# Another order of slots within a step of a two-layer transformer kernel

## The chip, the cores and the metric

The kernel runs on one core of one Trainium2 chip. The metric is device time in microseconds (us), the median of the runs. Engines are called as in the profile: PE is TensorE (PEld its weight loads), DVE is VectorE, ACT is ScalarE, POOL is GpSimd, SP is SyncE, whose queue issues nearly all DMAs.

## The reference

Two transformer blocks with adaptive layer norm run one after the other on x of 16 batches x 256 rows x 256 features, 16 heads of 16 features. Layer 0 is causal and gated by a condition, layer 1 has a key mask. Cut to what matters:

```python
# layer 0
xm = layernorm(x) * g * (1 + sc_a) + (be * (1 + sc_a) + sh_a)      # modulated
q, k, v = split(xm @ Wqkv)                                          # 16 heads of 16
attn = softmax(where(causal, q @ k.T * 16**-0.5, -inf))
x = x + gt_a * (merge(attn @ v) @ Wproj + bproj)
xm = modulate(layernorm(x)); x = x + gt_m * (gelu(xm @ W1 + b1) @ W2 + b2)
# layer 1: the same without causal mask and gates, with biases on q, k, v and a key padding mask
```

## The kernel before, in words

Everything stays on the chip. Each layer has an attention part, a software pipeline over the 16 batches, and an MLP part, a pipeline over 8 chunks of two batches. The attention part is a loop over steps t. In step t five batches are at work, each at another stage: n = t is normalised and transposed, a = t-1 gets its q, k and v, b = t-2 its scores (for the row maxima), c = t-3 its transposed scores, exponentials and half of its product with v, d = t-4 the rest of that product, the division by the row sums, the output projection and the residual. A full step thus does one batch's worth of each stage.

A step is 16 slots, one for each head. In every slot PE issues the scores of one head of b (lines 591 and 592, in layer 1 line 595) and the transposed scores of one head (lines 608 to 610, in layer 1 line 614). What else comes in a slot is set by the table SLOT and by PV_SLOT (the products with v, in slots 1, 5, 9, 13). Each engine's program is a fixed list in slot order; engines wait for each other by semaphores alone. An engine whose next instruction waits does nothing behind it.

The pieces that SLOT places, each of them on PE and then on the engines that read its bank:

- xT: four transposes of xn (line 648) into g_bank1. ACT applies scale and shift to half f=0 in the same slot and to half f=1 in the next slot (line 872, two instructions each, a full copy and a rounded one), and POOL then subtracts the rounded copy from the full one (line 1276, the low part of the operand). Both parts make xmT, which q, k and v of the next step read.
- q and k, two halves of six matmuls each (line 542), into g_bank1 and g_bank0; after the second half ACT rounds (line 819 or 823), DVE takes the low part (line 1054 or 1058), and SP copies both into q_stack or k_stack by six DMAs (line 407). The first matmul of q waits for xmT (semaphore xmT_ready).
- v, two halves of six, into g_bank1, copied by ACT (line 857).
- negmaxT: two transposes of the negated row maxima, copied by ACT (line 838), written into q_stack by SP.
- oT: two sets of four transposes (line 686) of the attention output, into g_bank0 and g_bank1; for each DVE takes the reciprocal of the sums and multiplies (lines 1126 and 1128).
- attnT: four transposes of the result (line 694), split by ACT (line 863) and DVE (line 1133).
- proj: two halves of six matmuls (line 542) with the output weights; DVE adds the bias (line 1138), POOL applies the gate and adds to x (lines 1257 and 1260).

The two g banks are handed from piece to piece; `take` waits until the piece that had the bank before has been read. The scores have three banks and the transposed scores two, so PE may run ahead of DVE and ACT by so much.

Of the kernel before, what the change touches and what calls it, by code (L numbers as in the profile page):

```python
# [27 lines left out]
LAYERS, B, T, D = 2, 16, 256, 256  # L28
H, HD = 16, 16
F = 4 * D  # L30
P = 128
NF, NM, NT = D // P, F // P, T // P
# [5 lines left out]
NG = H // GROUP  # L38
# [5 lines left out]
S_BANK = [h % 3 for h in range(H - 1)] + [1]  # L44
S_AGO = [next(k for k in range(1, H) if S_BANK[h - k] == S_BANK[h]) for h in range(H)]

SLOT = {"q": (0, 1), "negmaxT": 1, "k": (3, 5), "v": (6, 7), "oT": (8, 9), "attnT": 11, "xT": 12, "proj": (14, 15)}
PV_SLOT = [(LAG + 5 + GROUP * i) % H for i in range(NG)]

HALF = 3 * HD  # L50
# [40 lines left out]
def wait(eng, sem, value):  # L91
    if value is not None:
        eng.wait_ge(sem, value)
# [22 lines left out]
def build(nc, x_in, cond_in, mask_in, wa_in, w1_in, w2_in, ada0_in, ada1_in, cols_in, rows_in, ident_in,  # L116
          tri_in, out):
    fp32, f32r, bf16 = mybir.dt.float32, mybir.dt.float32r, mybir.dt.bfloat16
    ALU, ACT, AX = mybir.AluOpType, mybir.ActivationFunctionType, mybir.AxisListType

    with ExitStack() as ctx:
# [15 lines left out]
        ident = sb("ident", [P, P])  # L137
# [11 lines left out]
        xn = sb("xn", [P, 2, NT, D])  # L149
# [5 lines left out]
        negmax = sb("negmax", [P, 2, NT, 2, H], f32r)  # L155
        negmaxT = sb("negmaxT", [32, T], f32r)
        o_sb = sb("o_sb", [P, 2, NG, T])
# [340 lines left out]
        def _(pe):  # L498
# [40 lines left out]
            def product(dst, weights, rows, f, tiles):  # L539

                for n, (i, j) in enumerate(TERMS):
# [4 lines left out]

            USES = [("q", 1, 1, q_lo, 1), ("negmaxT", 0, 3, negmaxT_copied, 1), ("k", 0, 1, k_lo, 1),
                    ("v", 1, 1, v_copied, 1), ("oT0", 0, 4, attn_ready, 2), ("oT1", 1, 4, attn_ready, 2),
                    ("attnT", 0, 4, attnT_lo, 1), ("xT", 1, 0, xm_high, 1), ("proj", 0, 4, y_copied, 1)]

            BANK_OF = {u[0]: u[1] for u in USES}

# [80 lines left out]
            def step(layer, t):  # L633
                n, a, b, c, d = (t - k for k in range(5))
                gn, ga, gb, gc, gd = (in_layer(layer, s) for s in (n, a, b, c, d))
                for s in range(H):
                    if b.within(B):
                        scores(layer, gb, s)
                    if s < LAG and d.within(B):
                        scoresT(layer, gd, s + H - LAG)  # L640
                    if s >= LAG and c.within(B):
                        scoresT(layer, gc, s - LAG)
                    if s == SLOT["xT"] and n.within(B):
                        pe.wait_ge(xn_ready, gn.count(1, 1))
                        bank = take(layer, t, "xT")
                        for f in range(NF):
                            for i in range(NT):
                                last = transpose(bank[:, f * T + i * P:f * T + (i + 1) * P],
                                                 xn[:, gn.mod(2), i, f * P:(f + 1) * P], ident[:])
                        last.then_inc(xT_ready, 1)  # L650
                    if s == SLOT["negmaxT"] and c.within(B):
                        pe.wait_ge(negmax_ready, gc.count(1, 1))
                        bank = take(layer, t, "negmaxT")
                        for i in range(NT):
                            src = negmax[:, gc.mod(2), i].bitcast(fp32).rearrange("p e s -> p (e s)")
                            last = transpose(bank[0:32, i * P:(i + 1) * P], src, ident[:])
                        last.then_inc(negmaxT_ready, 1)
                    for name, first, ready in (("q", 0, q_ready), ("k", D, k_ready)):
                        if s in SLOT[name] and a.within(B):
                            m = SLOT[name].index(s)  # L660
                            if m == 0:
                                bank = take(layer, t, name)
                                if name == "q":
                                    pe.wait_ge(xmT_ready, ga.count(1, 1))
                                    pe.wait_ge(wa_split, 2 * layer + 1)
                            last = project(g_bank[BANK_OF[name]], ga, first, m)
                            if m == NF - 1:
                                last.then_inc(ready, 1)
                    if s in SLOT["v"] and a.within(B):
                        i = SLOT["v"].index(s)  # L670
                        if i == 0:
                            take(layer, t, "v")
                        bank = g_bank[BANK_OF["v"]]
                        for f in range(NF):
                            last = product(bank[:, i * D:(i + 1) * D],
                                           [xmT[:, ga.mod(2), e, f, i * P:(i + 1) * P] for e in range(2)],
                                           [wa[:, e, f, 2 * D:3 * D] for e in range(2)], f, NF)
                        if i == NT - 1:
                            last.then_inc(v_ready, 1)
                    if s in SLOT["oT"] and d.within(B):  # L680
                        i = SLOT["oT"].index(s)
                        if i == 0:
                            pe.wait_ge(o_copied, gd.count(NG, NG))
                        bank = take(layer, t, f"oT{i}")
                        for r in range(NG):
                            last = transpose(bank[:, r * P:(r + 1) * P], o_sb[:, gd.mod(2), r, i * P:(i + 1) * P],  # L686
                                             ident[:])
                        last.then_inc(oT_ready, 1)
                    if s == SLOT["attnT"] and d.within(B):
                        pe.wait_ge(attn_ready, gd.count(2, 2))  # L690
                        bank = take(layer, t, "attnT")
                        for f in range(NF):
                            for i in range(NT):
                                last = transpose(bank[:, f * T + i * P:f * T + (i + 1) * P],  # L694
                                                 attn[:, i, f * P:(f + 1) * P], ident[:])
                        last.then_inc(attnT_ready, 1)
                    if s in SLOT["proj"] and d.within(B):
                        i = SLOT["proj"].index(s)
                        if i == 0:
                            pe.wait_ge(attnT_lo, gd.count(1, 1))  # L700
                            take(layer, t, "proj")
                        bank = g_bank[BANK_OF["proj"]]
                        for f in range(NF):
                            last = product(bank[:, i * D:(i + 1) * D],
                                           [attnT[:, e, f, i * P:(i + 1) * P] for e in range(2)],
                                           [wa[:, e, f, 3 * D:4 * D] for e in range(2)], f, NF)
                        if i == NT - 1:
                            last.then_inc(proj_ready, 1)
                    if s in PV_SLOT:
                        r = PV_SLOT.index(s)  # L710
                        g, on = (gc, c) if LAG + 5 + GROUP * r < H else (gd, d)
                        if on.within(B):
                            attend(layer, g, r)
                    if s == SLOT["xT"] and t.const == ATTN_END:
                        chunk_transposes(layer, Step(0))
# [226 lines left out]
        def _(dve):  # L942
# [138 lines left out]
            def step(layer, t):  # L1081
# [3 lines left out]
                for s in range(H):  # L1085
# [26 lines left out]
                        row_statistics(layer, n)  # L1112
                    if s == SLOT["k"][1] and a.within(B):
                        low(layer, ga, k_hi, k_lo, g_bank[0], k_split, NF)
                    if s == 7 and n.within(B):
                        row_normalise(layer, n)
                    if s in SLOT["oT"] and d.within(B):
                        i = SLOT["oT"].index(s)
                        dve.wait_ge(oT_ready, gd.count(2, i + 1))
                        if i == 0:  # L1120
                            wait(dve, attnT_ready, gd.count(1))
                            if layer == 0 and d.const == 0:
                                dve.wait_ge(gates_stored, 16)
                        o = g_bank[i][:].rearrange("p (h n) -> p h n", n=32)
                        wait(dve, attn_ready, gd.count(2, i))
                        v.reciprocal(rsum[:, i], o[:, :, HD]).then_inc(rsum_ready, 1)
                        dve.wait_ge(rsum_ready, gd.count(2, i + 1))
                        v.tensor_tensor(attn[:, i].rearrange("p (h n) -> p h n", n=HD), o[:, :, 0:HD],
                                        rsum[:, i].unsqueeze(2).to_broadcast((P, H, HD)), ALU.mult)\
                            .then_inc(attn_ready, 1)  # L1130
                    if s == SLOT["attnT"] and d.within(B):
                        dve.wait_ge(attnT_hi, gd.count(1, 1))
                        v.tensor_tensor(attnT[:, 1], g_bank[0][:].rearrange("p (f n) -> p f n", f=NF), attnT[:, 0],
# [253 lines left out]
```

## Time and profile before

| | |
|---|---|
| median of 3 runs | 1167.23 us (1160.99 to 1169.55) |
| the profiled execution | 1161.7 us, span 1159.9 us |
| mean granted PE clock | 0.967 |
| PE busy | 1074.2 us (93%) |
| DVE, ACT, POOL busy | 787.0, 619.9, 252.6 us |

The span has four parts: attention of layer 0 to about 395 us, its MLP to about 606 us, attention of layer 1 to about 960 us, its MLP to the end. PE is busy almost throughout; a line of a timeline gives the start, the time taken, the engine, the line of the kernel, the operation, and in brackets the idle time ahead of it with what ended it. Starts of PE instructions that follow each other tell what each costs; their ends overlap the next ones.

### The profile page before, as it was taken

Reading aid. Unit: us, or ns where it says so; the run is one execution under the profiler, and the core shown is the slowest. Engines: PE = TensorE matmul, PEld = TensorE weight load, DVE = VectorE, ACT = ScalarE, POOL = GpSimd, SP = SyncE. Lnnn points to the kernel's source line nnn. Section 1 sums busy time; section 2 is a strip of 40 time slices with the busy share of each in tenths; the row PEclk is TensorE's granted clock in tenths of the full one; section 3 lists DMA queues with packets and bytes.
Section 4 is the critical chain, followed back from the end, with each engine's and each line's share of the span. In section 5 each row is a group of like instructions: output and inputs, shape, how many; then the busy total and the mean of one; then the engine's idle time right before and its main releaser. Section 6 shows DMA issues by size and latency. Waiting matters only on the chain.

```text
span 1159.9 us, 24601 instructions
## 1 busy us (share of the span) xinstructions
PE 1074.2 (93%) x8972; PEld 941.0 (81%) x8972; DVE 787.0 (68%) x2379; ACT 619.9 (53%) x1255; POOL 252.6 (22%) x253
## 2 busy tenths in 40 slices
PE   3879999999998789999975899999999987999998
PEld 3768888998886578998874788888888756988997
DVE  5568888888874577656635778878787746566553
ACT  1146667666664644433322677777777666334431
POOL 5111221312111342233321111121212013121111
PEclk9789999999998899999987899999999999999999
DMA  7657767575850100000056664736466400010001
GB/s 216 107 76 120 135 124 132 94 122 103 177 78 12 46 15 10 10 10 15 15 85 160 86 83 76 94 64 98 66 93 77 59 2 1 19 37 19 19 19 37
DMA packets 50832, 81.52 MB, mean 70 GB/s; under 512 B 8916, under 2 KB 23476, under 8 KB 49620
## 3 DMA queue, kind: packets, MB, share of 16 engines
q1 hardware_dynamic: 49752, 78.37, 38.2%
q10 hardware_dynamic: 960, 1.57, 1.2%
q8 instruction: 72, 1.18, 0.5%
q14 instruction: 48, 0.39, 0.2%
HBM read 22.64 MB, written 8.44 MB: 27 GB/s over the span
## 4 chain that ended last, share of the span: by engine, by line
PE 83%; DVE 4%; DMA 4%; SPq 2%; ACT 2%; issue 2%; POOL 2%; ACTq 1%; POOLq 0%; DVEq 0%
PE g_bank L542 14%; PE st_bank L542 13%; PE o_bank L628 9%; PE o_bank L542 8%; PE s_bank L542 7%; PE s_bank L595 6%; PE st_bank L614 5%; PE st_bank L608 4%; PE s_bank L591 3%; PE st_bank L610 3%; PE g_bank L686 2%; DMA k_stack<-qk_split 2%; SPq L407 2%; PE g_bank L694 1%; PE st_bank L609 1%
## 5 line engine op out<-in xcount | busy, mean ns | idle before, releaser
L806 ACT ACTIVATE probs<-st_bank 128x384 f32<-128x384 f32 (+1 forms) x512 | 273.4, 548 | 142.4 <-PE st_bank L610 81.7
L909 ACT ACTIVATE probs<-st_bank,cols 128x512 f32<-128x512 f32 x128 | 87.9, 689 | 217.8 <-PE st_bank L542 191.4
L542 PE MATMUL st_bank<-qk_split,q_stack 128*128 128x512 f32 x768 | 187.2, 402 | 14.5 <-ACT probs L909 10.9
L1099 DVE CUSTOM_DVE_ANT_0 s_bank<-s_bank,tri_wide 128x128 f32<-128x128 f32 (+1 forms) x512 | 170.3, 387 | 37.0 <-PE s_bank L592 35.8
L1105 DVE TENSOR_REDUCE maxima<-s_bank 128x2 f32<-128x512 f32 x256 | 168.7, 685 | 39.4 <-PE s_bank L595 38.6
L542 PEld LDWEIGHTS st_bank<-qk_split,q_stack 128*128 128x128 f32 x768 | 144.8, 191 | 51.9 <-ACT probs L909 14.0
L595 PE MATMUL s_bank<-k_stack,q_stack 97*128 97x256 f32 x512 | 115.2, 308 | 16.5 <-DMA k_stack<-mask_dram 9.4
L542 PE MATMUL g_bank<-xmT,wa 128*128 128x256 f32 x768 | 123.8, 301 | 4.8 <-POOL xmT L1276 4.8
L628 PE MATMUL o_bank<-probs,v_sb 128*32 128x256 f32 (+1 forms) x2048 | 124.5, 361 | 1.6 <-ACT probs L806 1.6
L595 PEld LDWEIGHTS s_bank<-k_stack,q_stack 97*128 97x128 f32 x512 | 79.8, 194 | 42.8 <-issue 25.9
L1276 POOL TENSOR_TENSOR xmT<-xm_full,xmT 128x512 fp32r<-128x512 f32 x32 | 42.3, 1322 | 320.3 <-ACT xmT L872 320.3
L542 PEld LDWEIGHTS g_bank<-xmT,wa 128*128 128x128 f32 x768 | 106.4, 202 | 5.7 <-issue 5.2
L614 PE MATMUL st_bank<-q_stack,k_stack 99*128 99x256 f32 x512 | 103.6, 286 | 3.1 <-DMA q_stack<-negmaxT 2.6
L591 PE MATMUL s_bank<-k_stack,q_stack 97*128 97x256 f32 x256 | 89.3, 350 | 9.8 <-DMA k_stack<-qk_split 6.4
L1202 DVE TENSOR_TENSOR wm_f32r<-probs,k_stack 128x512 fp32r<-128x512 f32 x128 | 92.7, 724 | 4.4
L542 PE MATMUL s_bank<-q_stack,k_stack 128*128 128x256 f32 x512 | 95.1, 284 | 0.0
L542 PE MATMUL o_bank<-q_stack,k_stack 128*128 128x256 f32 x512 | 94.8, 283 | 0.0
L608 PE MATMUL st_bank<-q_stack,k_stack 99*128 99x256 f32 x256 | 86.7, 340 | 4.6 <-DMA q_stack<-negmaxT 4.3
L628 PEld LDWEIGHTS o_bank<-probs,v_sb 128*32 128x32 f32 x2048 | 53.7, 110 | 43.0 <-issue 6.8
L614 PEld LDWEIGHTS st_bank<-q_stack,k_stack 99*128 99x128 f32 x512 | 79.2, 191 | 6.7 <-DMA q_stack<-negmaxT 3.2
L542 PEld LDWEIGHTS s_bank<-q_stack,k_stack 128*128 128x128 f32 x512 | 81.5, 192 | 0.0
L542 PEld LDWEIGHTS o_bank<-q_stack,k_stack 128*128 128x128 f32 x512 | 80.0, 189 | 0.0
(113 smaller groups left out, 2076.7 us busy)
## 6 DMA issues: line engine op xcount, KB each, us to landing
q_stack<-qk_split SPq DMA_DIRECT2D x192, 128.0 KB, 4.6
k_stack<-qk_split SPq DMA_DIRECT2D x180, 128.0 KB, 6.2
gate_rows<-gate_dram SPq DMA_DIRECT2D x32, 128.0 KB, 3.5
w_dram<-w_in SPq DMA_DIRECT2D x8, 512.0 KB, 7.0
wm_f32r<-w_dram SPq DMA_DIRECT2D x4, 1024.0 KB, 9.1
out<-x_sb SPq DMA_DIRECT2D x8, 512.0 KB, 2.9
x_sb<-x_in SPq DMA_DIRECT2D x4, 512.0 KB, 7.2
k_stack<-qk_split ACTq DMA_DIRECT2D x12, 128.0 KB, 8.4
```

Source lines behind the costliest of these rows:

```text
L542: last = mm(dst, weights[i], rows[j], start=(f == 0 and n == 0), stop=(f == tiles - 1 and n == len(TERMS) - 1))
L591: mm(bank[:, P:3 * P], q[:, P:T], k, start=True, stop=False)
L595: last = mm(bank[:, i * T:(i + 1) * T], q[:, i * P:(i + 1) * P], k, start=True, stop=True)
L608: mm(bank[:, 0:T], k[:, 0:P], q, start=True, stop=False)
L614: last = mm(bank[:, i * T:(i + 1) * T], k[:, i * P:(i + 1) * P], q, start=True, stop=True)
L628: last = mm(o_bank[32 * j:32 * j + 32, lo:T], v_sb[:, g.mod(VBUFS), kt, h, :], probs[:, h % 8, kt * T:kt * T + T - lo], start=(kt == 0), s ...
L806: activation(probs[:, h % 8, 0:n], st_bank[h % 2][:, 0:n], ACT.Exp, scale=SCALE)\
L909: activation(h_full[:, m % 2], st_bank[m % 2][:, :], ACT.Gelu, bias=cols[:, cb + m:cb + m + 1])\
L1099: last = v.tensor_tensor_reduce(out=bank[:, keys], in0=bank[:, keys], in1=tri_wide[:, T - (i + 1) * P:T], scale=1.0, scalar=LOWEST, op0=AL ...
L1105: v.reduce_max(maxima[:, gb.mod(2), :, slot], bank[:].rearrange("p (i n) -> p i n", n=T), AX.X).then_inc(max_done, 1)
L1202: v.tensor_tensor(hT[1][:, :, m], h, hT[0][:, :, m], ALU.subtract).then_inc(m_hT, 1)
L1276: g_.tensor_tensor(xmT[:, gn.mod(2), 1], xm_full[:], xmT[:, gn.mod(2), 0], ALU.subtract)\
```

## The change

The table SLOT is another one:

- q goes from slots 0 and 1 to 0 and 2, v from 6 and 7 to 4 and 6; k stays in 3 and 5, negmaxT in 1.
- oT goes from slots 8 and 9 to slot 7, both sets in a row; on DVE both divisions follow each other there, and row_normalise goes from slot 7 to slot 8.
- attnT goes from 11 to 9, proj from 14 and 15 to 11 and 12, xT from 12 to 13 (on ACT from 12 and 13 to 13 and 14).
- Where a slot has both, PE issues projections ahead of transposes.

No instruction is added or taken away, and SP's list of DMAs is the same.

```diff
-SLOT = {"q": (0, 1), "negmaxT": 1, "k": (3, 5), "v": (6, 7), "oT": (8, 9), "attnT": 11, "xT": 12, "proj": (14, 15)}
+SLOT = {"q": (0, 2), "negmaxT": 1, "k": (3, 5), "v": (4, 6), "oT": 7, "attnT": 9, "proj": (11, 12), "xT": 13}
...
-                    ("attnT", 0, 4, attnT_lo, 1), ("xT", 1, 0, xm_high, 1), ("proj", 0, 4, y_copied, 1)]
+                    ("attnT", 0, 4, attnT_lo, 1), ("proj", 0, 4, y_copied, 1), ("xT", 1, 0, xm_high, 1)]
...
+                    if s == SLOT["oT"] and d.within(B):
+                        pe.wait_ge(o_copied, gd.count(NG, NG))
+                        for i in range(NT):
+                            bank = take(layer, t, f"oT{i}")
+                            for r in range(NG):
+                                last = transpose(bank[:, r * P:(r + 1) * P],
+                                                 o_sb[:, gd.mod(2), r, i * P:(i + 1) * P], ident[:])
+                            last.then_inc(oT_ready, 1)
...
-                    if s == 7 and n.within(B):
+                    if s == SLOT["oT"] and d.within(B):
+                        for i in range(NT):
+                            dve.wait_ge(oT_ready, gd.count(2, i + 1))
...
+                    if s == 8 and n.within(B):
                         row_normalise(layer, n)
```

The first place is PE's list at the turn from one step to the next, in layer 0. These are the last instructions ahead of the first matmul of q (g_bank<-xmT,wa, which waits for xmT_ready) in the kernel before:

```order
L591 MATMUL s_bank<-k_stack,q_stack 128x256 [waits max_done]
L592 MATMUL s_bank<-k_stack,q_stack 128x128
L608 MATMUL st_bank<-q_stack,k_stack 128x256 [waits exp_done]
L609 MATMUL st_bank<-q_stack,k_stack 128x128
L610 MATMUL st_bank<-ident,tri 128x2x128
L542 MATMUL g_bank<-wa,attnT 128x256 x6
L591 MATMUL s_bank<-k_stack,q_stack 128x256 [waits max_done,k_stacked,q_stacked]
L592 MATMUL s_bank<-k_stack,q_stack 128x128
L608 MATMUL st_bank<-q_stack,k_stack 128x256 [waits exp_done]
L609 MATMUL st_bank<-q_stack,k_stack 128x128
L610 MATMUL st_bank<-ident,tri 128x2x128
L542 MATMUL g_bank<-xmT,wa 128x256 [waits wa_split,xmT_ready,xm_high]
```

And with the change:

```order
L610 MATMUL st_bank<-ident,tri 128x2x128
L591 MATMUL s_bank<-k_stack,q_stack 128x256 [waits max_done]
L592 MATMUL s_bank<-k_stack,q_stack 128x128
L608 MATMUL st_bank<-q_stack,k_stack 128x256 [waits exp_done]
L609 MATMUL st_bank<-q_stack,k_stack 128x128
L610 MATMUL st_bank<-ident,tri 128x2x128
L591 MATMUL s_bank<-k_stack,q_stack 128x256 [waits max_done,k_stacked,q_stacked]
L592 MATMUL s_bank<-k_stack,q_stack 128x128
L608 MATMUL st_bank<-q_stack,k_stack 128x256 [waits exp_done]
L609 MATMUL st_bank<-q_stack,k_stack 128x128
L610 MATMUL st_bank<-ident,tri 128x2x128
L542 MATMUL g_bank<-xmT,wa 128x256 [waits wa_split,xmT_ready,xm_high]
```

The projection's second half stood in slot 15 and no longer does; its first half has gone from slot 14 likewise, and the transposes of xn stand one slot nearer.

The second place is ACT's list around the scale and shift (xm_full and xmT), in layer 0. Before:

```order
L806 ACTIVATE probs<-st_bank 128x384 [waits pv_done,st_ready]
L872 ACTIVATE xm_full<-g_bank,table 128x256 [waits xmT_ready,v_ready,xT_ready]
L872 ACTIVATE xmT<-g_bank,table 128x256
L806 ACTIVATE probs<-st_bank 128x384 [waits pv_done,st_ready]
L872 ACTIVATE xm_full<-g_bank,table 128x256
L872 ACTIVATE xmT<-g_bank,table 128x256
L813 ACTIVATE o_sb<-o_bank 128x256 [waits pv_done]
```

With the change:

```order
L871 ACTIVATE xm_full<-g_bank,table 128x256 [waits xmT_ready,v_ready,xT_ready]
L871 ACTIVATE xmT<-g_bank,table 128x256
L812 ACTIVATE o_sb<-o_bank 128x256 [waits pv_done]
L805 ACTIVATE probs<-st_bank 128x384 [waits pv_done,st_ready]
L871 ACTIVATE xm_full<-g_bank,table 128x256
L871 ACTIVATE xmT<-g_bank,table 128x256
```

Between the two halves there now stand the copy of o_bank and the exponential of slot 14; before there was the exponential of slot 13 alone.

## Rows read from the trace of the kernel before

**Rows 1.** The page, part 1: busy time, share of the span, instructions.

```profile
PE 1074.2 (93%) x8972; PEld 941.0 (81%) x8972; DVE 787.0 (68%) x2379; ACT 619.9 (53%) x1255; POOL 252.6 (22%) x253
```

**Rows 2.** Windows of a full step, layer 0 and layer 1: length, busy by engine, PEclk.

```profile
224.28:244.47 20.19, 20.19 (x212) 18.13 (x211) 16.61 (x81) 13.41 (x29) 4.74 (x5) 1.00 0.69 114
...
755.62:775.78 20.16, 20.16 (x196) 17.22 (x195) 16.20 (x35) 15.05 (x32) 3.48 (x5) 1.00 0.53 81
```

**Rows 3.** Timeline, all engines, layer 0, from the transposes of xn to q.

```profile
240.02 0.60 PE L648 MATMUL g_bank<-ident,xn 128*128 128x128 f32 x4
...
241.09 0.86 PE L628 MATMUL o_bank<-probs,v_sb 128*32 128x256 f32 x16
...
241.57 0.48 ACT L806 ACTIVATE probs<-st_bank 128x384 f32<-128x384 f32 x1
...
241.88 0.39 PE L591 MATMUL s_bank<-k_stack,q_stack 97*128 97x256 f32 x1
241.94 0.57 ACT L872 ACTIVATE xm_full<-g_bank,table 128x256 f32<-128x256 f32 x1
...
242.39 0.28 PE L610 MATMUL st_bank<-ident,tri 128*128 128x256 bf16 x1
242.39 0.58 ACT L872 ACTIVATE xmT<-g_bank,table 128x256 fp32r<-128x256 f32 x1
242.43 0.96 PE L542 MATMUL g_bank<-wa,attnT 128*128 128x256 f32 x6
...
243.05 1.29 POOL L1276 TENSOR_TENSOR xmT<-xm_full,xmT 128x512 fp32r<-128x512 f32 x1 [10.98 <-ACT xmT L872]
...
243.23 0.28 PE L591 MATMUL s_bank<-k_stack,q_stack 97*128 97x256 f32 x1
...
244.93 0.36 PE L542 MATMUL g_bank<-xmT,wa 128*128 128x256 f32 x1
```

**Rows 4.** Timeline of PE, layer 0: transposes that are followed by a product with v.

```profile
236.56 0.60 PE L686 MATMUL g_bank<-ident,o_sb 128*128 128x128 f32 x4
237.09 0.86 PE L628 MATMUL o_bank<-probs,v_sb 128*32 128x256 f32 x16
```

**Rows 5.** Timeline, all engines, the same place in layer 1.

```profile
811.58 0.60 PE L648 MATMUL g_bank<-ident,xn 128*128 128x128 f32 x4
...
812.58 1.07 PE L628 MATMUL o_bank<-probs,v_sb 128*32 128x256 f32 x16
...
814.16 0.89 PE L542 MATMUL g_bank<-wa,attnT 128*128 128x256 f32 x6
...
814.82 1.29 POOL L1276 TENSOR_TENSOR xmT<-xm_full,xmT 128x512 fp32r<-128x512 f32 x1 [10.89 <-ACT xmT L872]
...
814.89 0.40 PE L595 MATMUL s_bank<-k_stack,q_stack 97*128 97x256 f32 x2
...
816.56 0.28 PE L542 MATMUL g_bank<-xmT,wa 128*128 128x256 f32 x1
```

**Rows 6.** Timeline of DVE, layer 0: the second division by the row sums.

```profile
237.45 0.25 DVE L1126 RECIPROCAL rsum<-g_bank 128x16 f32<-128x16 f32 x1
237.74 0.42 DVE L1128 TENSOR_TENSOR attn<-g_bank,rsum 128x256 f32<-128x256 f32 x1
```

**Rows 7.** Waits of PE over the span: us in total, times, longest us.

```profile
PE g_bank L648 <- ACT v_sb L857: 9.5, 2, 4.8
...
PE s_bank L591 <- DMA k_stack<-qk_split: 6.4, 2, 4.0
```

**Rows 8.** Windows around two short waits of PE; columns as in rows 2.

```profile
347.10:350.50 3.40, 1.86 (x24) 1.50 (x16) 2.39 (x15) 1.43 (x4) 1.75 (x2) 1.00 0.07 18
350.50:361.00 10.50, 10.17 (x68) 8.37 (x68) 5.09 (x24) 3.33 (x7) 0.00 (x0) 0.51 0.04 13
79.70:82.20 2.50, 0.10 (x2) 0.06 (x1) 1.37 (x8) 0.86 (x3) 1.17 (x1) 1.00 0.21 32
```

More of the change, by code:

```diff
@@ L642, in step @@
                         scoresT(layer, gc, s - LAG)
[L643 to L657, printed above, removed]
                     for name, first, ready in (("q", 0, q_ready), ("k", D, k_ready)):
@@ L679, in step @@
                             last.then_inc(v_ready, 1)
[L680 to L696, printed above, removed]
                     if s in SLOT["proj"] and d.within(B):
@@ L708, in step @@
                             last.then_inc(proj_ready, 1)
+                    if s == SLOT["negmaxT"] and c.within(B):
+                        pe.wait_ge(negmax_ready, gc.count(1, 1))
+                        bank = take(layer, t, "negmaxT")
+                        for i in range(NT):
+                            src = negmax[:, gc.mod(2), i].bitcast(fp32).rearrange("p e s -> p (e s)")
+                            last = transpose(bank[0:32, i * P:(i + 1) * P], src, ident[:])
+                        last.then_inc(negmaxT_ready, 1)
+                    if s == SLOT["oT"] and d.within(B):
[6 more added lines that the diff above has]
+                            last.then_inc(oT_ready, 1)
+                    if s == SLOT["attnT"] and d.within(B):
+                        pe.wait_ge(attn_ready, gd.count(2, 2))
+                        bank = take(layer, t, "attnT")
+                        for f in range(NF):
+                            for i in range(NT):
+                                last = transpose(bank[:, f * T + i * P:f * T + (i + 1) * P],
+                                                 attn[:, i, f * P:(f + 1) * P], ident[:])
+                        last.then_inc(attnT_ready, 1)
+                    if s == SLOT["xT"] and n.within(B):
+                        pe.wait_ge(xn_ready, gn.count(1, 1))
+                        bank = take(layer, t, "xT")
+                        for f in range(NF):
+                            for i in range(NT):
+                                last = transpose(bank[:, f * T + i * P:f * T + (i + 1) * P],
+                                                 xn[:, gn.mod(2), i, f * P:(f + 1) * P], ident[:])
+                        last.then_inc(xT_ready, 1)
                     if s in PV_SLOT:
@@ L1114, in step @@
                         low(layer, ga, k_hi, k_lo, g_bank[0], k_split, NF)
-                    if s == 7 and n.within(B):
-                        row_normalise(layer, n)
[L1117 to L1130, printed above, removed]
+                    if s == SLOT["oT"] and d.within(B):
+                        for i in range(NT):
+                            dve.wait_ge(oT_ready, gd.count(2, i + 1))
+                            if i == 0:
+                                wait(dve, attnT_ready, gd.count(1))
+                                if layer == 0 and d.const == 0:
+                                    dve.wait_ge(gates_stored, 16)
+                            o = g_bank[i][:].rearrange("p (h n) -> p h n", n=32)
+                            wait(dve, attn_ready, gd.count(2, i))
+                            v.reciprocal(rsum[:, i], o[:, :, HD]).then_inc(rsum_ready, 1)
+                            dve.wait_ge(rsum_ready, gd.count(2, i + 1))
+                            v.tensor_tensor(attn[:, i].rearrange("p (h n) -> p h n", n=HD), o[:, :, 0:HD],
+                                            rsum[:, i].unsqueeze(2).to_broadcast((P, H, HD)), ALU.mult)\
+                                .then_inc(attn_ready, 1)
+                    if s == 8 and n.within(B):
+                        row_normalise(layer, n)
                     if s == SLOT["attnT"] and d.within(B):
```

## The prediction, made before the result was known

> **What bounds the kernel now.** I read the page's part 1 first: PE is busy for 93% of the span, the next engine for 68% [rows 1]. Then the windows of one full step in each layer: in 20.19 us PE is busy for 20.19, in layer 1 for 20.16 of 20.16, at full clock [rows 2]. So a steady step has no wait on PE at all, and its length is the sum of what PE issues. The change adds and removes nothing there. It can gain only at the fill and the drain of the two pipelines and in the small gaps between unlike instructions; it can lose wherever the new order asks for something before it is ready. So I went through the timeline of one step, piece by piece, asking for each piece how long before its use it is ready, and how much of PE's work now stands between.
>
> **The place that decides: xT to q.** Before, the transposes of xn start at 240.02, and q, which reads their modulated result, at 244.93 [rows 3]: PE has 4.91 us of other work in between. The chain beside it (ACT f=0, f=1, then POOL) ends with POOL's subtraction at 243.05 + 1.29 = 244.34. That is 4.32 us after the transposes' start and only 0.59 us before q. In layer 1 the distance is 816.56 - 811.58 = 4.98 and the chain ends at 816.11, 0.45 us ahead [rows 5]. So the cover is nearly used up already.
>
> The change takes cover away. Between xT and q there are no longer the scores of slot 13 and no longer the two projection halves:
> - transposes to the product with v: 241.09 - 240.02 = 1.07 before [rows 3]; now it follows at once, and that spacing is 0.53 (237.09 - 236.56) [rows 4]: -0.54;
> - two projection halves, 243.23 - 242.43 = 0.80 each [rows 3]: -1.60;
> - scores right behind a projection start their partner some 0.09 sooner than behind others (the scores and transposed scores of a slot take 242.43 - 241.88 = 0.55 [rows 3], against 0.46 behind a projection, which is what is left of the 4.91): two such places go, +0.18.
>
> That leaves 2.95 us of cover. In layer 1: 4.98 - (812.58 - 811.58 - 0.53) - 2 x (814.89 - 814.16) = 3.05 [rows 4, 5].
>
> The chain also gets longer, since ACT keeps its order. Half f=1 now stands behind the exponential of slot 14, and that waits for PE's slot 14. Counted from the transposes' start in layer 0: product with v at 0.53, first scores of slot 14 at 0.53 + (241.88 - 241.09) = 1.32; the last transposed score starts 0.51 later and takes 0.28 [rows 3], 2.11; the exponential starts at 2.15 and frees ACT 0.37 later (241.94 - 241.57), 2.52; the two instructions of f=1 end 242.39 + 0.58 - 241.94 = 1.03 later, 3.55; POOL starts 0.08 later (243.05 against 242.97) and ends at 4.92; q can start at about 4.97. PE is there at 2.95. **Wait: 2.0 us in every full step of layer 0.** In layer 1 the product with v takes 1.0 and the wider exponential half a us of ACT, and the same walk ends at about 5.25 against 3.05: **2.2 us**. If the exponential did not delay it, the old chain of 4.32 + 0.05 would still leave 1.4 in layer 0; that is the lower bound, for 24 steps 34 us.
>
> How many steps: xT of batch n and q of n meet at 16 step turns in each layer. At the first ones the pipeline is filling and PE waits there for other things, k's copies at the first scores among them [rows 7], which come before q and cover the chain. I count 12 turns in each layer: 12 x 2.0 + 12 x 2.2 = **+50 us**.
>
> **The other pieces.**
> - oT to attnT. Eight transposes in slot 7, attnT two slots later. DVE needs 0.60 + 0.03 for the first set, and for each division 237.74 + 0.42 - 237.45 = 0.71 [rows 6]: 2.05 us after the first transpose. PE's own work to that place is 0.72 for the eight transposes and some 1.15 for two sets of scores, 1.87, and in layer 1 about 1.76. Wait 0.2 to 0.3 us in some 30 steps: **+7**. Zero to 14 as bounds.
> - v to oT in g_bank1: ACT's copy of v ends just before the second oT set starts. Nothing to 0.1 a step; taken as 0.
> - attnT to proj. ACT and DVE have to split attnT before slot 11. By adding their times behind the transposes I find DVE ready within 0.1 us of PE in layer 0 and earlier in layer 1. 0.
> - Gaps between unlike instructions: the two 0.09 of above are lost and as many gained elsewhere, and the two oT sets stand in one place; summed over the 16 slots I get a step 0.08 us shorter, an estimate. **-2**. With zero and -5 as bounds.
> - q and k later. q's second half is in slot 2, and half of v precedes k's second half, one block of 0.80 [rows 3] that did not stand there. So SP copies k later by about as much, and the next step's first scores, which need it, may have to wait up to that long. In full steps this costs nothing, since those scores come half a us ahead of q: what they wait, q's own wait is shorter by. While the pipeline fills there is no such cover, and PE already waits there for k, 6.4 us in two places of layer 0 [rows 7]; four such turns in both layers, at 0.8 to 0.9: **+3**.
> - First step of each layer: v's first half now waits for q's split before k's second half is issued, so k and, behind ACT's DMA issues for it, v's copy are late; PE waits for that copy (9.5 us in two places) [rows 7]. Two blocks of 0.80 each: **+3**.
> - Ends of the layers: the MLP's first transposes come behind the projection instead of ahead of it, the division ahead of the chunk's normalisation, the bias addition earlier. About +1 each, **+2**, between -4 and +6.
>
> Without the clock the sum is 50 + 7 - 2 + 3 + 3 + 2 = **+63 us**.
>
> **The clock.** PE's granted clock has two levels, 2.4 and 1.2 GHz. A wait in a stretch in which PE was busy for 1.86 of 3.40 us was followed by 10.5 us at 0.51 although PE was busy for 10.17 of them; one of 2.4 us (busy 0.10 of 2.50) by none, the clock staying at 1.00 [rows 8]. So waits of 2 us are on the edge. I take something over half of the 24 waits, 14, to cost a low spell of about a third of that one, 3.4 us at half speed or 1.7 us of lost work: **+24**. Bounds: nothing, and 24 spells of twice that length, 82. The Trainium skill, TensorE: Matmul & The Clock Gate, section "HAM oscillation", describes a kernel in which a wait in every turn of the loop drops the clock in every turn and pays for the warm-up each time. By that rule all 24 would drop; rows 8 show one wait of each outcome.
>
> Sum: 1161.7 of the profiled execution + 63 + 24 = 1248.7; I say 1248. The profiled execution lies 5.5 us below the median of the runs shown, inside their spread of 8.6.
>
> **Rivals.**
> 1. *Every turn drops the clock, or for longer* (0.13). For it: the rest of the stretch around the wait is light, only scores. Against: the 2.4 us wait without a drop. 24 spells of 1.7 to 3.4 us: 1161.7 + 63 + 41 to 82 = 1266 to 1307.
> 2. *The waits are shorter* (0.12): ACT's half f=1 is not held by the exponential, or the clock never falls. Lower bound 1161.7 + 34 + 13 = 1209, to 1225 with full waits and full clock.
> 3. *The chain stays hidden, and the time is not longer* (0.07; 0.03 of it below -1%). Then only the ends count: bias addition earlier, no wait of negmaxT for its bank, -2 from the gaps, -4 at the layer ends, and the filling as before: 1155 to 1165. This decides if the modulated operand is ready within 2.95 us of the transposes, where it took 4.32. It would need ACT and POOL together to save 1.4 us; nothing in the change shortens POOL's 1.29 or ACT's four instructions. I give it little.
>
> The forecast has 0.68, for 1225 to 1266.
>
> **The numbers.** Likeliest 1248. Range 1209 to 1288: it leaves out rival 3 and the upper half of rival 1. About 1% (some 12 us) is what a measurement of this kernel can tell from no change. Faster 0.03, same 0.04, slower 0.93.
>
> **What would show it.** In the profile after, q's first matmul (g_bank<-xmT) has an idle time of about 2 us in each full step, ended by POOL's xmT, some 48 us in total, the largest entry among PE's waits. A full step takes about 22.3 us. attnT's transposes wait 0.1 to 0.3 for DVE's attn. Part 2 shows PEclk dips spread over both attention parts. If q has no such wait, the forecast is wrong; if it has and the steps are at full clock, only the clock term was.

## The result, and the profile after

The changed kernel takes 1285.16 us (median of 4 runs, 1281.81 to 1291.51), the kernel before, measured beside it, 1164.76 (median of 4): a ratio of 1.103, with an interval of 1.099 to 1.107. It is slower by 120 us. The profiled executions have spans of 1283.7 and 1159.9 us; the one of before is one of the kernel's faster ones, so what is read from the two traces adds up to 123.8 us.

First the busy times from the page of the profile, which answer to [rows 1], then waits of PE (engine, line, releaser: us in total, times, longest us), which answer to [rows 7]:

```profile
PE 1141.3 (89%) x8972; PEld 973.6 (76%) x8972; DVE 792.5 (62%) x2379; ACT 626.7 (49%) x1255; POOL 251.0 (20%) x253
```

```profile
PE g_bank L542 <- issue: 39.3, 24, 1.8
PE g_bank L705 <- ACT v_sb L856: 11.3, 2, 5.9
...
PE s_bank L591 <- DMA k_stack<-qk_split: 8.6, 2, 5.8
...
PE g_bank L697 <- DVE attn L1125: 7.0, 18, 1.2
...
PE g_bank L542 <- DVE qk_split L1057: 3.8, 14, 1.1
```

PE stands still ahead of g_bank (the first matmul of q) 24 times, at most 1.8 us. The view names no releaser and says "issue", but the timeline shows for what PE waits. These are all engines in layer 0, from the transposes of xn (now line 705) to q; they answer to [rows 3]:

```profile
202.93 0.60 PE L705 MATMUL g_bank<-ident,xn 128*128 128x128 f32 x4
...
203.57 0.56 ACT L871 ACTIVATE xm_full<-g_bank,table 128x256 f32<-128x256 f32 x1
...
205.09 0.49 ACT L805 ACTIVATE probs<-st_bank 128x384 f32<-128x384 f32 x1 [0.22 <-PE st_bank L610]
205.47 0.56 ACT L871 ACTIVATE xm_full<-g_bank,table 128x256 f32<-128x256 f32 x1
...
206.57 1.26 POOL L1275 TENSOR_TENSOR xmT<-xm_full,xmT 128x512 fp32r<-128x512 f32 x1 [13.14 <-ACT xmT L871]
...
207.93 1.04 PE L542 MATMUL g_bank<-xmT,wa 128*128 128x256 f32 x6 [1.69 <-issue]
```

ACT stands idle for 0.22 us ahead of the exponential of slot 14, whose scores PE has only just made; half f=1 follows at 205.47; POOL ends at 207.83; q starts at 207.93, 5.00 us after the transposes. The forecast of the chain was 4.97. From the last transposed score (start 205.96) PE would have gone on 0.04 us later, so the wait takes 1.9 us; the view counts 1.69, because it begins a wait only at the modelled end of the matmul ahead.

The windows of the same execution: one full step of layer 0 (answers to [rows 2]), then the wait, what follows it, and the rest.

```profile
184.44:208.78 24.34, 22.53 (x214) 19.24 (x213) 16.70 (x80) 13.54 (x29) 4.83 (x6) 0.93 0.60 95
206.20:208.70 2.50, 0.81 (x7) 0.80 (x7) 1.17 (x7) 1.05 (x3) 2.13 (x2) 0.99 0.00 0
208.70:212.10 3.40, 3.40 (x26) 2.09 (x25) 0.74 (x4) 1.00 (x3) 1.64 (x2) 0.51 0.00 0
212.10:215.00 2.90, 2.90 (x28) 2.90 (x27) 1.67 (x8) 1.71 (x4) 0.00 (x0) 1.00 0.20 57
```

A step of 20.19 us has become one of 24.34: 22.6 with the 1.7 us that the low clock costs in it taken off, where 22.3 was forecast without the clock. Right behind the wait PE, busy all the time, runs at 0.51 of its clock, that is at 1.2 GHz, for 3.4 us, and then at 2.4 GHz again.

Where the time went is read by cutting both spans at the same instructions: the first scores of t = 5 and of t = 17 bound the 12 full steps of a layer. Before (start:end in us, length, busy PE, PEld, DVE, ACT, POOL, PEclk, DMA share, GB/s):

```profile
102.50:345.10 242.60, 242.23 (x2517) 217.26 (x2517) 198.05 (x954) 159.33 (x344) 54.78 (x57) 1.00 0.69 120
345.10:396.50 51.40, 41.86 (x387) 33.90 (x385) 24.78 (x104) 27.61 (x65) 8.88 (x8) 0.87 0.03 8
396.50:607.80 211.30, 197.36 (x1253) 176.61 (x1253) 128.99 (x266) 82.37 (x148) 71.48 (x64) 0.98 0.14 28
...
675.00:916.40 241.40, 241.40 (x2326) 206.18 (x2325) 192.98 (x403) 179.03 (x369) 39.56 (x46) 1.00 0.58 82
916.40:962.20 45.80, 36.56 (x351) 26.84 (x349) 23.62 (x54) 30.78 (x65) 5.04 (x5) 1.00 0.01 3
```

And after:

```profile
108.50:399.80 291.30, 270.58 (x2517) 231.93 (x2517) 198.71 (x950) 160.76 (x345) 56.84 (x60) 0.92 0.59 100
399.80:452.60 52.80, 40.24 (x385) 32.20 (x384) 25.62 (x107) 28.42 (x66) 7.18 (x7) 0.92 0.09 26
452.60:669.90 217.30, 203.27 (x1253) 180.82 (x1253) 129.11 (x265) 82.48 (x149) 71.54 (x64) 0.95 0.11 23
...
736.10:1032.90 296.80, 270.04 (x2327) 217.85 (x2325) 195.37 (x404) 183.87 (x372) 41.19 (x47) 0.93 0.48 67
1032.90:1084.40 51.50, 38.29 (x348) 28.29 (x348) 24.22 (x55) 31.25 (x65) 3.77 (x4) 0.95 0.01 3
```

The spans are those of one execution each. Full steps: +48.7 in layer 0 and +55.4 in layer 1, 104 of the 123.8 us. The other 20: the filling of layer 0 +6.0, the first MLP with layer 1's first two steps +6.0, layer 1's draining +5.7, the rest +2. ("Filling" is the part up to the first full step, "draining" that behind the last.) In the full steps a mean clock of 0.92 over 291.3 us and 0.93 over 296.8 means 47 and 42 us at half speed, so 23 + 21 = 44 us of lost work. What is left of the 104 is 60 us of waits, 47 of them idle time by these windows. Read from the starts of PE's instructions, 44 of the 60 are the 24 waits at q, and 16 are smaller ones elsewhere, 8 of them ahead of attnT and 3.5 ahead of v's first half in layer 1.

### The profile page after: what moved, and what is told of

Read it like the earlier page. It is cut to its first block, busy times and chain, and to the rows that moved or that the text cites. A ratio compares the mean times of both kernels' runs of the same rounds, so it can differ in the third digit from the quotient of the medians.

```text
span 1283.7 us, 24601 instructions
## 1 busy us (share of the span) xinstructions
PE 1141.3 (89%) x8972; PEld 973.6 (76%) x8972; DVE 792.5 (62%) x2379; ACT 626.7 (49%) x1255; POOL 251.0 (20%) x253
## 4 chain that ended last, share of the span: by engine, by line
PE 72%; DVE 7%; issue 7%; DMA 5%; ACT 4%; SPq 3%; POOL 1%; ACTq 1%; POOLq 0%; DVEq 0%
PE g_bank L542 14%; PE st_bank L542 13%; PE o_bank L628 9%; PE o_bank L542 7%; PE s_bank L542 7%; PE s_bank L595 3%; PE st_bank L614 3%; PE s_bank L591 3%; DMA k_stack<-qk_split 3%; PE st_bank L608 3%; SPq L407 3%; DVE attn L1125 2%; PE st_bank L610 2%; PE g_bank L697 2%; DMA q_stack<-negmaxT 1%
## 5 line engine op out<-in xcount | busy, mean ns | idle before, releaser
L542 PE MATMUL st_bank<-qk_split,q_stack 128*128 128x512 f32 x768 | 194.5, 413 | 17.7 <-DVE q_stack L969 9.1
L542 PEld LDWEIGHTS st_bank<-qk_split,q_stack 128*128 128x128 f32 x768 | 150.0, 198 | 57.3 <-ACT probs L908 12.6
L542 PE MATMUL g_bank<-xmT,wa 128*128 128x256 f32 x768 | 131.3, 313 | 44.1 <-issue 39.3
L542 PEld LDWEIGHTS g_bank<-xmT,wa 128*128 128x128 f32 x768 | 113.4, 215 | 48.5 <-issue 48.5
L628 PE MATMUL o_bank<-probs,v_sb 128*32 128x256 f32 (+1 forms) x2048 | 136.7, 389 | 1.6 <-ACT probs L805 1.6
L595 PE MATMUL s_bank<-k_stack,q_stack 97*128 97x256 f32 x512 | 116.7, 312 | 15.4 <-DMA k_stack<-mask_dram 8.1
L595 PEld LDWEIGHTS s_bank<-k_stack,q_stack 97*128 97x128 f32 x512 | 82.7, 200 | 45.2 <-issue 33.4
L614 PE MATMUL st_bank<-q_stack,k_stack 99*128 99x256 f32 x512 | 106.9, 294 | 4.4 <-DMA q_stack<-negmaxT 3.8
L591 PE MATMUL s_bank<-k_stack,q_stack 97*128 97x256 f32 x256 | 90.6, 354 | 11.8 <-DMA k_stack<-qk_split 8.6
L628 PEld LDWEIGHTS o_bank<-probs,v_sb 128*32 128x32 f32 x2048 | 56.7, 116 | 55.1 <-issue 23.9
L608 PE MATMUL st_bank<-q_stack,k_stack 99*128 99x256 f32 x256 | 89.4, 351 | 4.4 <-DMA q_stack<-negmaxT 4.1
L614 PEld LDWEIGHTS st_bank<-q_stack,k_stack 99*128 99x128 f32 x512 | 81.9, 197 | 8.9 <-DMA q_stack<-negmaxT 4.6
```

The source lines that it names most:

```text
L542: last = mm(dst, weights[i], rows[j], start=(f == 0 and n == 0), stop=(f == tiles - 1 and n == len(TERMS) - 1))
L591: mm(bank[:, P:3 * P], q[:, P:T], k, start=True, stop=False)
L595: last = mm(bank[:, i * T:(i + 1) * T], q[:, i * P:(i + 1) * P], k, start=True, stop=True)
L608: mm(bank[:, 0:T], k[:, 0:P], q, start=True, stop=False)
L614: last = mm(bank[:, i * T:(i + 1) * T], k[:, i * P:(i + 1) * P], q, start=True, stop=True)
L628: last = mm(o_bank[32 * j:32 * j + 32, lo:T], v_sb[:, g.mod(VBUFS), kt, h, :], probs[:, h % 8, kt * T:kt * T + T - lo], start=(kt == 0), s ...
```

## The experiments

**e1: xT back to an earlier slot.** One number of the table:

```diff
-SLOT = {"q": (0, 2), ..., "oT": 7, "attnT": 9, "proj": (11, 12), "xT": 13}
+SLOT = {"q": (0, 2), ..., "oT": 7, "attnT": 9, "proj": (11, 12), "xT": 11}
```

> The changed kernel with one number undone: the transposes of xn (xT) in slot 11 instead of 13; all else as in the changed kernel. Theory A (the loss is the wait of q for the modulated operand, and the low clock that this wait brings): in layer 0 PE's work from xT to q is 4.8 us again, the chain of ACT and POOL 4.4, so the wait is gone in full steps, and with it the low spells. Left are the small terms (attnT waiting for DVE, fill and drain of the layers): 1170 to 1190 us. Theory B (the new order itself costs: oT twice in one slot, attnT two slots later, v and q apart, and PE's changed mixture): most of the loss stays, over 1230 us.

1202.46 us, ratio to before 1.032 (1.026 to 1.038): of the 120 us one number gives back 83, but 37 are left, more than theory A had (1202 against 1170 to 1190). The full steps, both layers:

```profile
108.90:359.40 250.50, 247.46 (x2516) 218.46 (x2516) 201.15 (x951) 160.32 (x344) 55.78 (x59) 1.00 0.69 117
...
696.70:952.60 255.90, 249.58 (x2324) 206.53 (x2324) 199.83 (x403) 182.39 (x370) 40.22 (x46) 1.00 0.56 77
```

No low clock, no wait at q, but 8 us above before in layer 0 and 14.5 in layer 1. The timeline of PE in a full step of layer 1 shows why:

```profile
824.85 0.47 PE L595 MATMUL s_bank<-k_stack,q_stack 97*128 97x256 f32 x2 [0.45 <-DMA k_stack<-qk_split]
...
831.20 0.97 PE L542 MATMUL g_bank<-wa,xmT 128*128 128x256 f32 x6 [0.16 <-DVE qk_split L1057]
...
838.27 0.66 PE L697 MATMUL g_bank<-ident,attn 128*128 128x128 f32 x4 [0.23 <-DVE attn L1125]
```

Three small waits: the first scores for k's copies, v's first half for the low part of q, attnT for DVE's second division. The last is in every full step; from 720 to 960 us the view lists 11 of it, 7 of the second and 3 ahead of the first scores. They cost more than their idle time. attnT starts 0.52 us behind the transposed scores where it was 0.12 before, and in layer 0, where the view shows no wait, 0.41 instead of 0.12: over 24 steps 8 of the 22 us.

**e2: xT in slot 12**, the same number as 12.

> The changed kernel with xT in slot 12 instead of 13. Theory A: cover of 3.5 us against a chain of 4.4 (half f=1 waits for the exponential of slot 13, which is early), so a wait of 0.9 to 1.0 us at 24 turns, 23 us, with few or no low spells of the clock: 1195 to 1225 us. Theory B: as the changed kernel within 10 us, over 1265.

1223.37 us, ratio 1.048 (1.040 to 1.055), inside theory A's range; its full steps are 258.0 and 264.1 us long, at full clock. Against e1 that is 7.5 and 8.2 us for twelve turns, 0.65 each, where 0.9 to 1.0 was expected. From the transposes to q it takes 4.40 us in layer 0 (the chain was put at 4.4). That part of it takes the place of e1's waits for k and for negmaxT is likely, but not shown by a run of its own.

**e3: the second half of the scale and shift moved up on ACT.**

```diff
-                    if s in (SLOT["xT"], SLOT["xT"] + 1) and n.within(B):
-                        f = s - SLOT["xT"]
+                    for f in range(NF) if s == SLOT["xT"] and n.within(B) else ():
                         if f == 0:
```

> The changed kernel, with both halves of the scale and shift on ACT in slot 13, so that half f=1 no longer stands behind the exponential of slot 14. PE's order is untouched. Theory A with the exponential as part of the chain: the chain shrinks from 4.97 to about 4.0 us in layer 0, the wait from 2.0 to about 1.05, and the clock falls less often: 1200 to 1240 us. If the chain's length is set by ACT's and POOL's work alone: no change within 8 us of the changed kernel. Theory B: no change either.

1222.56 us, ratio 1.050 (1.044 to 1.056). PE's program is the changed kernel's, instruction for instruction; only ACT no longer keeps half f=1 behind the exponential of slot 14. That alone is worth 63 us, since with the shorter waits the clock also stays up:

```profile
109.40:370.20 260.80, 251.13 (x2517) 218.93 (x2517) 214.04 (x952) 160.23 (x345) 56.71 (x60) 1.00 0.66 112
704.70:969.80 265.10, 254.69 (x2325) 207.15 (x2324) 211.91 (x404) 182.98 (x371) 41.52 (x47) 1.00 0.54 75
```

From the transposes to q it now takes 4.02 us instead of 5.00, as expected. What PE still waits there comes in two pieces, since the exponential of slot 14 is late in its turn; PE's timeline in a full step of layer 0:

```profile
219.34 0.38 PE L608 MATMUL st_bank<-q_stack,k_stack 99*128 99x256 f32 x1 [0.45 <-ACT probs L805]
...
220.08 0.94 PE L542 MATMUL g_bank<-xmT,wa 128*128 128x256 f32 x6 [0.17 <-issue]
```

By the starts the first piece costs 0.6 us (219.34 against 218.67 and 0.06) and the second 0.4 (220.08 against 219.63 and 0.04). e2 has the same two pieces, of 0.4 us each.

**e4: matmuls without use in q's wait.**

```diff
                                 if name == "q":
+                                    for _ in range(10 if t.const >= 2 else 0):
+                                        mm(bank[:, 0:T], wa[:, 0, 0, 0:P], wa[:, 0, 0, 0:T],
+                                           start=True, stop=True)
                                     pe.wait_ge(xmT_ready, ga.count(1, 1))
```

> The changed kernel, with ten matmuls of 128x256 that compute nothing of use put ahead of q's wait for xmT, into the bank that q then overwrites. They run in the time in which PE would stand still, between ACT's last half (xm_high) and POOL's subtraction, some 1.3 us. The wait as such is as long as before. Clock theory (46 us of the loss are low spells that the idle time brings): the low spells in the full steps go, PEclk is near 0.97 again, the time falls by 35 to 46 us to 1240 to 1250 us. If the low clock is not due to the idle time: unchanged or, by the extra matmuls, longer, 1285 to 1300 us.

1250.35 us, ratio to before 1.073 (1.068 to 1.079), at the upper edge of the clock theory: 35 us less than the changed kernel, with 120 matmuls more in each layer's full steps:

```profile
109.30:381.00 271.70, 265.37 (x2637) 233.22 (x2637) 199.22 (x953) 160.85 (x346) 57.27 (x60) 1.00 0.64 108
719.70:998.60 278.90, 269.01 (x2444) 221.80 (x2445) 195.07 (x403) 183.62 (x371) 41.68 (x47) 1.00 0.51 71
```

PEclk is 1.00, the waits for xmT are still there under another name (PE now waits for ACT ahead of the ten, and for POOL behind them; from the transposes to q it is 4.99 us, as before), and the full steps are 19.6 and 17.9 us shorter. So the low spells came from PE standing still, and they are a cost by themselves: 37 us measured, 44 computed from the clock. Where the other 7 went is not shown.

**e5: undoing two of e1's three waits.**

```diff
-SLOT = {"q": (0, 2), ..., "attnT": 9, "proj": (11, 12), "xT": 13}
+SLOT = {"q": (0, 1), ..., "attnT": 10, "proj": (12, 13), "xT": 11}
```

> The changed kernel with xT in 11 (as e1), and further q back in slots 0 and 1, attnT in 10, the projection in 12 and 13. e1 left 37 us. If these are the three waits that e1's full steps in layer 1 show (first scores for k's copies, v's first half for q's split, attnT for DVE's division, 0.2 to 0.6 us each), the last two go: 12 x 0.7 us in layer 1 and some 3 us in layer 0, against e1 10 to 14 us less, 1188 to 1193 us; the wait for k stays, since half of v still stands ahead of k's second half. If the full steps lose by the mixture of PE's work, no change against e1: 1198 to 1206 us.

1200.54 us, ratio 1.031 (1.028 to 1.033): no gain over e1. The time lies where the second reading had it, but that reading is not shown by it, for two waits did go (attnT starts 0.12 us behind the scores again) and the waits of PE in the full steps are other ones, first in layer 0, then in layer 1:

```profile
PE st_bank L608 <- DMA q_stack<-negmaxT: 3.5, 10, 0.4
```

```profile
PE st_bank L614 <- DMA q_stack<-negmaxT: 1.8, 10, 0.2
PE g_bank L542 <- DVE attnT L1132: 1.7, 11, 0.2
```

With q's second half in slot 1 ahead of negmaxT, as the new code orders them, PE reaches the transposed scores of slot 4 sooner after negmaxT than SP's copy of the maxima lands; and with one slot between attnT and the projection, DVE's split is late. A test of three waits had made two new ones.

**e6: the kernel before with q and v alone as in the change.**

```diff
-SLOT = {"q": (0, 1), "negmaxT": 1, "k": (3, 5), "v": (6, 7), ...}
+SLOT = {"q": (0, 2), "negmaxT": 1, "k": (3, 5), "v": (4, 6), ...}
```

> The kernel before with only q and v moved as in the change (q in 0 and 2, v in 4 and 6); everything else where it was. If k's and q's lateness is worth what e1 shows: the first scores wait 0.5 us for k in layer 1's full steps and v's first half 0.3 us for q's split, 12 x 0.8 = 10 us, some 3 us in layer 0, and about 5 us while the pipelines fill: 1180 to 1187 us. As the prediction had it (nothing for a full step by itself, +6 for the filling): 1168 to 1172 us.

1186.95 us, ratio 1.019 (1.015 to 1.022): 22 us, at the upper end of the first expectation and far from the second, the prediction's. The four runs lie at 1181 to 1183 and at 1191 to 1192, and the profiled one is of the slower pair. Full steps and, in layer 1, their waits:

```profile
105.00:353.40 248.40, 244.40 (x2516) 217.08 (x2516) 196.55 (x955) 158.63 (x344) 54.85 (x57) 1.00 0.70 118
691.70:945.60 253.90, 246.71 (x2324) 206.52 (x2325) 193.08 (x403) 179.08 (x368) 39.59 (x45) 1.00 0.56 78
```

```profile
PE s_bank L595 <- DMA k_stack<-qk_split: 2.0, 4, 0.8
PE s_bank L595 <- DMA k_stack<-mask_dram: 1.9, 3, 0.8
PE g_bank L542 <- DVE qk_split L1058: 1.3, 8, 0.2
```

The full steps are 5.8 and 12.5 us longer than before; the order of q and v is a cost of its own.

**e7: the kernel before with xT alone one slot later**, 12 to 13.

> The kernel before with only xT moved one slot later, 12 to 13; the projection stays in 14 and 15. Then PE has 0.53 + 0.79 + 0.55 + 0.80 + 0.46 + 0.79 + 0.46 = 4.4 us from xT to q, and the chain, held by the exponential of slot 14, takes 5.0: a wait of 0.6 us at 24 turns, 14 us, and no low spells: 1176 to 1184 us. If instead cover and chain were not additive like this (if the projection's leaving is what matters), no change within 5 us of the kernel before.

1184.13 us, ratio 1.016 (1.014 to 1.019), at the upper end of the expectation. Its full steps are 249.7 and 251.9 us, 0.59 and 0.88 a step above before, where 0.6 was worked out, at full clock. From the transposes to q it takes 5.01 us, and in most turns of layer 0 PE's wait there costs 0.64. With the projection still behind it, moving xT from slot 12 to 13 costs 19 us; in the changed kernel the same move (e2 to the changed kernel) costs 62.

**e8: the kernel before, PE kept busy while layers drain.**

```diff
+                    if s == 3 and t.const in (B + 1, B + 2):
+                        bank = take(layer, t, "v")
+                        for _ in range(14):
+                            mm(bank[:, 0:T], wa[:, 0, 0, 0:P], wa[:, 0, 0, 0:T], start=True, stop=True)
```

> The kernel before with 14 matmuls that compute nothing of use in slot 3 of the two draining steps of each layer (t = 17 and 18), where PE stands still for 1.6 to 1.9 us until the row maxima's DMA lands. If idle time there is what brings the low spell of 10 us at 351 us, that spell goes and with it up to 5 us: ratio 0.995 to 0.998. If it does not: no change or up to 1 us longer.

1162.63 us, ratio 0.998 (0.996 to 1.0003): the interval just holds no change. The trace shows the mechanism: where before there were 10.5 us at 0.51 [rows 8], and layer 0's draining took 51.4 us, there is now

```profile
348.50:395.10 46.60, 40.72 (x414) 33.83 (x412) 24.18 (x104) 27.64 (x65) 8.89 (x8) 0.96 0.03 9
```

4.8 us less. In that execution the filling of layer 0, where the program is that of before, took 3.6 us longer with more low clock (0.82 against 0.88), and the first MLP's stretch 3 us longer, so a gain over the whole kernel is not shown. Two executions can differ by as much in parts that are the same. No version that was run beats the kernel before beyond its interval.

## Why the prediction was right, and where its sizes were off

**xT to q: right, mechanism and size.** The chain was put at 4.97 and 5.25 us and measures 5.00 and 5.27 in the two layers; PE is there 2.0 us sooner, in layer 1 too, where 2.2 was forecast; 24 turns. A few of them are shorter, the first 0.9, so the sum is 44 us by the starts, against 50. The sign that was named ahead came: q's wait is the largest entry among PE's waits, 39.3 us by the view against some 48. e3 shows that the exponential of slot 14 is part of the chain, not only ACT's and POOL's own work, and e7 that cover and chain add up slot by slot. e1 shows that this place carries 83 us of the 120, clock included.

**The clock: right in kind, too small.** 14 of 24 turns were taken to drop it, for +24 us. Windows of 5 us behind each of the 24 waits show a low clock in 21. In layer 0 it is all twelve; in layer 1 every fourth turn from the first one on stays at full speed and the one behind it drops for longer. Of the 21 spells 16 last 3.4 us and 5 twice as long. Two turns, one without and one with a drop:

```profile
738.80:743.80 5.00, 5.00 (x48) 4.20 (x49) 1.50 (x3) 2.82 (x7) 1.09 (x1) 1.00 0.02 7
...
762.00:767.00 5.00, 4.98 (x29) 3.27 (x30) 0.69 (x1) 1.00 (x3) 1.15 (x1) 0.50 0.02 6
```

The waits themselves do not differ. The first of these two was followed by no drop, the second by a long one:

```profile
738.75 0.47 PE L542 MATMUL g_bank<-xmT,wa 128*128 128x256 f32 x2 [1.80 <-issue]
...
960.00 1.62 PE L542 MATMUL g_bank<-xmT,wa 128*128 128x256 f32 x6 [1.80 <-issue]
```

The price is 44 us by the clock and 37 by e4. This is the term that was mis-sized, by 13 to 20 us: 14 spells of 1.7 us of lost work were taken, and there were 21, five of them of 3.4. Rival 1, every turn or for longer, was nearer to it. One wait of 2.4 us that had done nothing [rows 8] was too little to halve the number by. Whether light work around the wait is the reason, as rival 1 had it, no run shows. The Trainium skill, TensorE: Matmul & The Clock Gate, section "HAM oscillation", tells of a kernel whose clock drops in every turn of its loop; the trace agrees in 21 of 24. The waits of that kernel are longer, some 3 to 5 us by the page, so the page does not say, as the prediction took it, that all 24 waits of 2 us would drop the clock; that 21 of them do is what this trace shows.

**q and k later: put at nothing in a full step, which holds at most under q's wait.** e6 has q and v moved by themselves at 6 and 12.5 us for the two layers' full steps. That k's lateness is hidden behind q's wait fits e2, which costs 8 us over e1 where the wait alone would be 11, but is not isolated. But the wait of v's first half for q's low part was overlooked as one of every full step; it comes after q and nothing covers it. In the changed kernel it shows as 3.8 us in 14 waits, first steps included. So this term of the prediction, nothing in a full step, failed.

**oT to attnT**: +7 forecast. The starts give 0.3 us in each full step of layer 0 and 0.4 in layer 1, 8 us over 24 steps, for 0.2 to 0.3 in some 30 forecast. That the view's sum for this wait is 7.0 us, in 18 places, is luck: 3.8 of it, in 2 places at the ends of the layers, stood in the kernel before. No experiment isolates what it costs the kernel; e5 was to, and did not.

**Filling, first steps, ends of layers**: +8 forecast, 20 measured. The filling of layer 0 is 6.0 us longer. But e8's execution is 3.6 us longer there with an unchanged program, so much of that may be chance. PE waits 5.8 us at most for k's copies, where it was 4.0 [rows 7], and 5.9 for v's copy, where it was 4.8. In the first MLP's stretch the clock is 0.95 of full instead of 0.98, about 6 us of lost work by itself. It is not low around the wait for v's copy (last row) more than before (0.88), but where the MLP begins:

```profile
452.60:470.00 17.40, 14.16 (x42) 10.51 (x43) 12.84 (x30) 9.02 (x20) 10.41 (x12) 0.75 0.08 28
470.00:500.00 30.00, 27.44 (x157) 23.52 (x156) 20.14 (x34) 11.49 (x19) 12.18 (x8) 0.89 0.03 9
...
640.00:669.90 29.90, 22.04 (x152) 20.95 (x150) 8.96 (x21) 7.71 (x16) 6.04 (x7) 0.89 0.52 81
```

Which wait brings that is open. At the end of each attention part PE waits 4.5 us for the MLP's first operand, where it was 1.2 and 2.3, since the chunk's transposes now stand behind the projection, and I had allowed 1.

Sum: forecast 1248, measured 1285. Of the 37 us between them 20 are the clock in full steps, 12 the ends, and 5 what is left of 11 us more in small waits and 6 less at q. A part of the 12 can be chance.

## What to carry to other kernels

When a full step has no idle time on the bound engine, no reordering of it can gain there more than the small gaps between unlike instructions; ask of each piece how long before its use it is ready, and subtract from that what the new order takes out between. Walk the chain on every engine that keeps its order: an instruction that has moved behind another one's wait is late by that wait. And where PE waits in every turn, price the wait twice, once as it stands and once as the low clock behind it. One wait of that length that did nothing is no proof against it: here 21 did it and 3 did not.

## What the runs showed of the hardware

Two us of standing still cost almost four: 2.0 of wait, and behind it, in 21 of 24 turns, 3.4 us at 1.2 GHz, which is 1.7 us of work (in five turns twice that). Ten matmuls of no use in the gap made the kernel 35 us faster. A wait of mostly 0.6 to 0.8 us in every turn (e7), or two of 0.4 to 0.6 us within 1.5 us (e2 and e3, layer 0), left the clock of the full steps at 1.00 throughout. In layer 1 the drops come in a pattern of three turns with and one without, for a step of unchanged content and waits of the same 1.80 us by the view, so what a given wait does also depends on something besides its length, perhaps on when it falls.
